# A DLRM tower on one core: the order of turns and lookups, who rounds the table halves, and how ids are compared

## The reference, cut to what matters

```python
e = jnp.stack([tbl_0[ids[:, 0]], ..., tbl_25[ids[:, 25]]], axis=1)
T = jnp.concatenate([r_dense[:, None, :], e], axis=1)          # 2048 x 27 x 128
Z = jnp.einsum('bnd,bmd->bnm', T, T)
z = Z[:, iu0, iu1]                                             # 351 pairs above the diagonal
h = jnp.concatenate([z, r_dense], axis=1)
h = jnp.maximum(h @ W_top1 + b_top1, 0.0)                      # 512
h = jnp.maximum(h @ W_top2 + b_top2, 0.0)                      # 256
y = h @ W_top3
```

## Time and profile before

| | us |
|---|---|
| median of 3 runs | 503.87 |
| lowest, highest | 503.16, 509.52 |
| the profiled execution's own time | 503.01 |
| its span, first to last instruction | 501.2 |
| PE busy (matmul) | 394.7 (79%) |
| POOL busy | 251.3 (50%) |
| DVE busy | 221.8 (44%) |
| ACT busy | 175.2 (35%) |
| mean granted TensorE clock | 0.884 of 2.4 GHz |

### The profile page before, as it was taken

The page is one execution under the profiler, slowest core; times in us unless marked ns, Lnnn a source line. Parts: engine busy times, 40 slices in busy tenths (PEclk is TensorE's granted clock), DMA queues, the critical chain, the costliest instruction groups (busy, mean ns, idle before and its releaser), DMA issues.

```text
span 501.2 us, 9930 instructions
## 1 busy us (share of the span) xinstructions
PE 394.7 (79%) x4044; PEld 348.3 (69%) x4044; DVE 221.8 (44%) x815; ACT 175.2 (35%) x220; POOL 251.3 (50%) x263
## 2 busy tenths in 40 slices
PE   5848357696498968987689868989679866999998
PEld 3727356595397837976489746978479754988987
DVE  5616642586263404823365404734247223744321
ACT  4121550354135312363215512354214522344231
POOL 6747573637545554447635563546653475360000
PEclk9958596888599969999699976999599996999999
DMA  8926130115501422115311332114321251013221
GB/s 216 245 60 192 48 105 24 52 48 128 171 25 47 97 71 90 38 33 140 102 27 38 81 100 85 33 43 105 99 60 28 50 130 47 24 47 67 49 51 22
DMA packets 45878, 39.07 MB, mean 78 GB/s; under 512 B 32930, under 2 KB 39113, under 8 KB 45834
## 3 DMA queue, kind: packets, MB, share of 16 engines
q1 hardware_dynamic: 36014, 21.40, 16.4%
q0 software_dynamic: 8192, 16.79, 13.0%
q10 hardware_dynamic: 1628, 0.25, 0.3%
HBM read 32.40 MB, written 6.02 MB: 77 GB/s over the span
## 4 chain that ended last, share of the span: by engine, by line
PE 52%; another core or an unknown queue 27%; DVE 11%; ACT 4%; issue 4%; DMA 1%; DVEq 0%; SPq 0%; ACTq 0%
PE look_ps L763 24%; PE gram_ps L790 9%; PE mlp_ps L810 7%; DVE hot L474 7%; PE look_ps L773 5%; ACT T L625 3%; PE mlp_ps L820 3%; PE look_ps L754 1%; DVE gram L497 1%; DVE tab_lo L456 1%; PE look_ps L831 1%; PE look_ps L853 1%; DMA ids_all<-in_ids_dram 1%; DVE gram L445 0%
## 5 line engine op out<-in xcount | busy, mean ns | idle before, releaser
L425 POOL DMA_INDIRECT rows<-in_tbl_dram,ids_all x240 | 233.9, 975 | 193.3 <-PE look_ps L773 104.5
L474 DVE TENSOR_SCALAR hot<-ids_near 125x256 fp32r<-125x256 f16 x640 | 146.0, 300 | 142.8 <-remote 98.7
L763 PE MATMUL look_ps<-hot,tab_hi 125*128 125x256 f32 x616 | 160.6, 298 | 29.1 <-DVE hot L474 11.1
L763 PE MATMUL look_ps<-hot,tab_lo 125*128 125x256 f32 x616 | 156.4, 291 | 6.8 <-issue 6.0
L763 PEld LDWEIGHTS look_ps<-hot,tab_hi 125*128 125x128 f32 x616 | 122.1, 198 | 33.0 <-issue 26.6
L763 PEld LDWEIGHTS look_ps<-hot,tab_lo 125*128 125x128 f32 x616 | 122.5, 199 | 8.5 <-issue 8.5
L625 ACT COPY T<-look_ps 128x384 f32<-128x384 f32 (+1 forms) x80 | 83.4, 1076 | 113.0 <-PE look_ps L773 96.8
L790 PE MATMUL gram_ps<-T 128*54 128x54 f32 x2048 | 72.7, 224 | 39.3 <-issue 30.1
L790 PEld LDWEIGHTS gram_ps<-T 128*54 128x54 f32 x2048 | 64.3, 138 | 51.3 <-issue 39.6
L617 ACT COPY T<-look_ps 128x512 f32<-128x512 f32 x32 | 38.5, 1204 | 100.9 <-PE look_ps L763 53.5
L497 DVE COPY gram<-gram_ps 128x486 f32<-128x486 f32 (+1 forms) x64 | 37.9, 607 | 77.3 <-remote 52.7
(11 more groups left out here) (74 smaller groups left out, 151.4 us busy)
## 6 DMA issues: line engine op xcount, KB each, us to landing
dots<-gram SPq DMA_DIRECT2D x28, 182.2 KB
ids_near<-ids_rows SPq DMA_DIRECT2D x7, 640.0 KB
rows<-in_tbl_dram,ids_all POOLq DMA_INDIRECT x240
T<-in_tbl_dram SPq DMA_DIRECT2D x5, 448.0 KB
pairs<-dots SPq DMA_DIRECT2D x14, 117.0 KB
rows<-in_r_dense_dram SPq DMA_DIRECT2D x16, 64.0 KB
gram<-in_tbl_dram SPq DMA_DIRECT2D x2, 448.0 KB
pairs<-dots SPq DMA_DIRECT2D x7, 104.0 KB
```

What stands on the lines that cost most here:

```text
L425: pool.indirect_dma_start(rows[:, t % 2, place[n], :], None, tables[n - 1], bass.IndirectOffsetOnAxis(ap=index[:, n - 1:n].bitcast(U32), a ...
L474: eq = nc.vector.tensor_scalar(hot[:VP, at % 2, c], ids_near[:VP, u % 2, k], float(c), None, ALU.is_equal)
L763: mm = pe.matmul(dst, w[:VP, k, c], hot[:VP, slot, c], start=(c == 0 and half == 0), stop=(c == CH - 1 and half == 1))
```

## The change

Three edits.

1. In `first_half`, ACT's loop and PE's loop, for u > 0: turn(u,1,2) now comes between look(u+1,0) and look(u+1,1), turn(u,1,3) between look(u+1,1) and look(u+1,2), and turn(u,1,4) after layer1 steps 0 to 8. Unit 0's order is unchanged, but for the casts.
2. `lead`, `top` and its semaphore are gone. ACT casts raw to `tab_hi` itself (its write rounds), in the order LEADING and sooner; DVE subtracts `tab_hi` from raw. There are five raw slots in place of three, so eight tables load at once, and the small weights load later.
3. For units 2 and up, places 0, 6, 7, 8 and 9 are compared by one TENSOR_TENSOR of 8x256 elements against eight chunk numbers kept in PSUM (columns 500 to 507 of `gram_ps`'s second bank, memset once). So that PE doesn't write that bank meanwhile, piece 1 of products(u, l) waits for the compares before it.

```diff
+    LEADING = (0, 1, 2, 3, 4, 6, 5, 7, 8, 9)
-        raw_slots = [table_at(spare, 0), table_at(spare, CH * D), table_at(gram_flat, 2 * CH * D)]
+        raw_slots = [table_at(spare, i * CH * D) for i in range(2)] + [table_at(gram_flat, i * CH * D) for i in range(3)]
+        steps = gram_ps[:, 1, 500:500 + CH]
+        def by_steps(u, at):
+            return u >= 2 and at in (0, 6, 7, 8, 9)
         def first_half(u):
             if u > 0:
-                return [("turn", u, 1, 0), ("turn", u, 1, 1), ("look", u + 1, 0), ("look", u + 1, 1),
-                        ("turn", u, 1, 2), ("look", u + 1, 2), ("turn", u, 1, 3), ("turn", u, 1, 4)]
+                return [("turn", u, 1, 0), ("turn", u, 1, 1), ("look", u + 1, 0), ("turn", u, 1, 2),
+                        ("look", u + 1, 1), ("turn", u, 1, 3), ("look", u + 1, 2), ("turn", u, 1, 4)]
...
-            for k in range(6):
+            for k in range(8):
                 load_raw(k)
             load_dense(0, 0)
-            load_raw(6)
-            load_small_weights()
-            load_raw(7)
+            load_raw(8)
...
+            def split(k):
+                dve.wait_ge(hi_ready, hi_count(k))
                 for c in range(0, CH, 2):
                     minus = nc.vector.tensor_tensor(tab_lo[:VP, k, c:c + 2], raw[k][:VP, c:c + 2],
-                                                    top[2 if k in WHOLE else i % 2][:VP, c:c + 2], ALU.subtract)
+                                                    tab_hi[:VP, k, c:c + 2].bitcast(F32), ALU.subtract)
...
+                if by_steps(u, at):
+                    if u == 2 and at == 0:
+                        dve.wait_ge(steps_ready, CH)
+                    near = ids_near[:VP, u % 2, k:k + 1].to_broadcast([VP, CH, Q])
+                    eq = nc.vector.tensor_tensor(hot[:VP, at % 2], near, steps[:VP].rearrange(
+                        "p (c q) -> p c q", q=1).to_broadcast([VP, CH, Q]), ALU.is_equal)
...
             def hi_out(k):
-                i = split_count(k) - 1
-                act.wait_ge(top_ready, i + 1)
-                nc.scalar.copy(tab_hi[:VP, k], top[2 if k in WHOLE else i % 2][:VP]).then_inc(hi_ready, 1)
+                act.wait_ge(raw_landed[k], 32)
+                nc.scalar.copy(tab_hi[:VP, k], raw[k][:VP]).then_inc(hi_ready, 1)
...
+                if t == 0 and b == 0:
+                    pe.wait_ge(steps_ready, CH)
+                if b == 1 and 0 < u < END:
+                    pe.wait_ge(hot_ready, K * (u + 1) + (1 if l == 0 else 8))
...
                 turn(u, 1, 1)
                 look(u + 1, 0)
+                turn(u, 1, 2)
+                look(u + 1, 1)
+                turn(u, 1, 3)
                 if u > 0:
-                    look(u + 1, 1)
-                    turn(u, 1, 2)
                     look(u + 1, 2)
                     layer1(u - 1, 0, 8)
-                    turn(u, 1, 3)
-                    layer1(u - 1, 8, 12)
                     turn(u, 1, 4)
-                    layer1(u - 1, 12, 16)
+                    layer1(u - 1, 8, 16)
```

More of the change, by code:

```diff
@@ L95, in dlrm_tower @@
     assert VP * CH == V and VP <= P and V <= 2048 and D == P and F1C == 4 and F2C == 2 and K % 2 == 0
-    assert NV % 2 == 1 and MC * PC == NV and KP <= P and 18 * NV <= 512 and dense_round == NR - 1
+    assert NV % 2 == 1 and MC * PC == NV and KP <= P and 18 * NV <= 500 and dense_round == NR - 1
     w1_pieces = pair_weight_pieces(NV, HALF, MC)
@@ L150, in dlrm_tower @@
         in_turn = [k for k in range(K) if k not in WHOLE]
-        raw = [whole_raw[WHOLE.index(k)] if k in WHOLE else raw_slots[in_turn.index(k) % 3] for k in range(K)]
-        top = [table_at(gram_flat, 0), table_at(gram_flat, CH * D)]
+        raw = [whole_raw[WHOLE.index(k)] if k in WHOLE else raw_slots[in_turn.index(k) % len(raw_slots)] for k in range(K)]
         look_ps = psum("look_ps", [P, RING, 512], F32)
@@ L187, in dlrm_tower @@
         dense_ready = sem("dense_ready")
+        steps_ready = sem("steps_ready")
         gram_done = sem("gram_done")
@@ L307, in load_raw @@
             def load_raw(k):
-                if k not in WHOLE and in_turn.index(k) >= 3:
-                    sp.wait_ge(lo_ready, in_turn.index(k) - 2)
+                if k not in WHOLE and in_turn.index(k) >= len(raw_slots):
+                    sp.wait_ge(lo_ready, in_turn.index(k) - len(raw_slots) + 1)
                 src = tables[onehot[k]].rearrange("(p c) d -> p c d", c=CH)
@@ L472, in compare @@
                     dve.wait_ge(hot_looked, K * u + at - 1)
-                for c in range(CH):
-                    eq = nc.vector.tensor_scalar(hot[:VP, at % 2, c], ids_near[:VP, u % 2, k], float(c), None,
-                                                 ALU.is_equal)
+                if by_steps(u, at):
[4 more added lines that the diff above has]
+                        "p (c q) -> p c q", q=1).to_broadcast([VP, CH, Q]), ALU.is_equal)
+                else:
+                    for c in range(CH):
+                        eq = nc.vector.tensor_scalar(hot[:VP, at % 2, c], ids_near[:VP, u % 2, k], float(c), None,
+                                                     ALU.is_equal)
                 eq.then_inc(hot_ready, 1)
@@ L545, in _ @@
                 compare(0, at)
+            dve.wait_ge(ids_t_ready, UNITS)
+            for c in range(CH):
+                nc.vector.memset(steps[:, c:c + 1], float(c)).then_inc(steps_ready, 1)
             compare(1, 0)
@@ L555, in _ @@
                 if u == 0:
+                    split(WHOLE[0])
                     dense_out(u, 1)
[L557 to L562, removed]
+                compare(u + 1, 6)
+                compare(u + 1, 7)
+                if u > 0:
                     dense_out(u, 1)
@@ L565, in _ @@
                 if u == 0:
-                    lead(WHOLE[1])
-                    compare(u + 1, 7)
-                    rest(WHOLE[1])
+                    split(WHOLE[1])
                 compare(u + 1, 8)
                 if u == 0:
-                    lead(WHOLE[2])
+                    split(WHOLE[2])
                 compare(u + 1, 9)
-                if u == 0:
-                    rest(WHOLE[2])
                 if u + 2 < UNITS:
@@ L667, in _ @@
                 spread_out(j)
-            hi_out(0)
+            for k in LEADING[:5]:
+                hi_out(k)
             look_out(0, 0)
-            hi_out(2)
             for g in range(4):
```

62 lines of the change are left out of this document (18 added, 44 removed).

## The result

The changed kernel takes 532.44 us (median of 4 runs, 530.51 to 536.64); the kernel before, beside it, 506.69 (503.16 to 511.29). The ratio is 1.051, with a 95% interval of 1.043 to 1.059: slower, as forecast, and 5.4 us above the 527 us of the prediction. Ratios here leave out executions that took over 1.5% more than the fastest of their kernel; medians keep them. The profiled execution took 530.51 us, with a span of 528.7 us and a mean granted clock of 0.848, where it was 0.884.

What follows compares the result with a forecast made beforehand. Prediction: no engine is full; PE's signals come late while POOL gathers without a pause. Profiled 503.0 + 26 (turns) - 1.4 (compares) - 1 (split) = 526.6, forecast 527 us; own range 515 to 535, 8 in 10 488 to 537.

Steps and rivals of the forecast that it cites:

- Edit 1: First half of units 1 to 6: sooner turns join POOL's rounds 1 and 2; +4.3 us a unit, +26 us, bounds -18 and +38.
- X: Start of POOL's round 1 in a unit's first half, 255.44 us in the forecast's trace; later times count from it.
- the products' 3.0 us: Lateness of the signal for the products' first copy, first half; forecast to go, already inside the +4.3 us a unit.
- unit 0's unknown wait: Unit 0, before the fifth compare: 5.96 us idle behind eight gathers; the forecast took unit 0's times as price.
- Edit 3: Five TENSOR_TENSOR compares: +0.4 to 0.5 us each, hidden; gathers beside compares get faster, 0.24 us a run, -1.4 us in all.
- The covers: Compares of places 6 and 7 hide behind layer1, 8 and 9 under the 14-gather run; without cover, 2 us a unit.
- Edit 2: Start of the kernel: `lead` leaves DVE, which waits for late signals anyway; -1 us, bounds -4 and +2.
- The sum: Whole kernel: 503.0 + 26 - 1.4 - 1 = 526.6 us, forecast as 527 us, 4.6% slower.
- A: Third lookup's signal, first half: not late in the new order, only the products' 3.0 us go; 484 us, chance 0.17.
- B: First half: signal late, but the clock holds and POOL pauses sooner; 508 to 512 us, no tellable change, chance 0.20.
- C: Second half: 2-port compares cause the late signals, so removing them gains 10 us or more a unit; 445 us, chance 0.05.
- D: Place 4's late compare delays y and layer1; slow clock covers layer1 and part of the products; 540 us, chance 0.08.

Runs made afterwards that it cites:

- split and compares: Changed kernel without the sooner turns (ACT rounds leading parts, five compares by TENSOR_TENSOR), against the kernel before, chip 9: 513.85 us, ratio 1.0147.
- the split alone: Kernel before with only ACT rounding the leading parts and five raw slots: 515.80 us, ratio 1.0167 on chip 9; 357.25 us, 0.9841 on chip 4.

## Why the prediction was right, and where it was not

**The verdict, the sign and the cause held.** The forecast was 527 us with slower as the likeliest, from one mechanism: eight gathers in a row in the first half, and the third table's signal late because of them. The run without gathers takes away all late signals behind the start, and the hold on POOL, with the turns left in their new places, takes away two thirds of their loss and puts the third table's signal back in its old place. Both bear out the mechanism on chips like that of the forecast's trace.

**Edit 1** was priced at +4.3 us a unit, X to the products' first copy going from 23.3 to 27.6 us. In unit 3 it went to 295.18 - 268.84 = 26.3 us, +3.0; the mean of units 1 to 6 is 25.9, +2.6. By its own steps in unit 3: the fifth compare was due at X + 11.5 and came at X + 10.0; the couple was to take 6.55 us and took 6.41; the products' 3.0 us were to go and went. The 1.5 us too many came from taking unit 0's unknown wait as it stood. This wait came in two sizes: some 4.5 us in five of the six units and 5.9 in one, but 5.7 to 5.9 in four of the six in the turns alone. The unit as a whole lost 3.8 us, so about 1 of it lies outside that stretch. Six units at 3.8 are 23 us for the 26 of the forecast. The turns alone, on chip 9, cost 19.4 us by the medians (529.22 - 509.85), 3.2 a unit.

**Edit 3** was priced at -1.4 us. The instruction takes 2.29 us for the 2.2 forecast. The 14-gather run, from its first start to its last, went from 16.49 us (282.09 to 298.58) to 16.26 (298.50 to 314.76), about the 0.24 forecast. The covers held as well. Places 8 and 9 are compared under the run, from 300.69 us. The late compare, at 316.52 us, is that of place 0 of the next unit; it takes 0.58 us more (2.29 - 1.71), but DVE then still waits 0.80 us for ACT's dense vector, as it waited 0.67 before, so this is on no path either. Whether the 1.4 us came can't be told: with split and compares against the split alone the ratios are 1.0147 and 1.0167. No run has the compares alone on such a chip; on chip 4 they lose 0.3%.

**Edit 2** is the step that failed: "I take -1 us; bounds -4 and +2". On the forecast's own two traces it is +5.7 us at tile 4, and alone on chip 9 it costs 1.67%, some 8 us. The text had a right ground for no gain, that DVE waits there for late signals anyway. But the term was written down as one of work, with bounds from work, and the start was never walked through as the loop was: neither where POOL pauses there nor when the stored ids release it. Both moved; which of them made the loss is open.

**The sum**, 23 + 6 from 503.0 us, is 532; the profiled execution took 530.5. A term too large by 3 and one too small by 7 left 4 us against the 526.6 of the text. On chip 9 it is the same by medians: +19.4 for the turns and +8.2 for the split. So that the number came within 5.4 us is in part luck, two errors that pull against each other.

**The rivals.** A (484 us, the lateness is unit 0's own) falls: the fifth compare is late in all of units 1 to 6, by a wait of 4.5 us or more. B (508 to 512, POOL pauses sooner and the clock holds) falls by the clock of 0.59 and by the missing pause; only with POOL held by hand did the kernel come to 511.65. C (445 us, the 2-port compares are the cause) falls: five of ten compares left that form, and the long wait is 11.35 us for 12.61, and 0.72 of this difference is that the two compares in front of it take 4.49 us for 3.77; and where all ten compares keep it but 240 gathers are gone, no signal is late behind the start. The Trainium skill (SBUF — State Buffer, "Who interferes with whom") says that such a compare and a GpSimd instruction lock each other out, whichever comes second, and that PE never waits. The traces agree in direction: most gathers beside the old compares take about 1.02 us for 0.95, in five units of the changed kernel one takes 2.4, and the 34 beside the new compares all take 0.95. But these are delays of POOL's, and it is PE's signals that are late, with or without the old compares. D (540 us, the slow clock covers layer1) falls in unit 3, where layer1 takes 3.46 us for 16 matmuls, at the fast clock.

## What to carry to other kernels

Before a step is moved sooner, ask what it releases: here a turn that was done sooner let another engine's gathers close up into one run, and that cost 4%, where the turn's new place gives 0.4% on a chip without late signals. A pattern read from one chip's trace can be right there and absent on another; when a quarter of the chain is "unknown", measure on more than one chip before tuning to it. And a term that is priced by the work it removes must still be asked whether it moves a pause.

## What the runs showed of the hardware

The same program takes 362.4 us on chip 4 and 508 to 516 on the others, some 29% less, with the same work: PE 4044 matmuls, POOL 256 gathers. Edits 1 and 2 change sign between them (0.9955 and 0.9841 against 1.0396 and 1.0167). The changed kernel itself was not run on chip 4.

On the other chips it is not only signals that come late: PE's own instructions drip, too. Under the run of 14 gathers of the kernel before, PE's lookups run at full pace until 291 us; from 292 us single matmuls follow each other with idle time between them that no wait explains, until 300.6 us, a microsecond after the run:

```profile
293.50 0.38 PE L773 MATMUL look_ps<-ident,rows 128*128 128x128 f32 x2 [1.02 <-issue]
```

Two timelines of PE beside POOL's first run of gathers, the changed kernel and then the split alone on chip 4, the same 16 matmuls of one look:

```profile
22.63 0.38 PE L740 MATMUL look_ps<-hot,pairs 125*128 125x256 f32 x1 [1.62 <-issue]
24.73 0.59 PE L740 MATMUL look_ps<-hot,pairs 125*128 125x256 f32 x1 [1.72 <-issue]
26.13 0.58 PE L740 MATMUL look_ps<-hot,pairs 125*128 125x256 f32 x1 [0.82 <-issue]
```

```profile
18.32 3.62 PE L740 MATMUL look_ps<-hot,pairs 125*128 125x256 f32 x16
```

In the changed kernel a matmul starts every 1.4 to 2.1 us; PE is back at its pace at 35 us, some 3.5 us after POOL's last gather of that run has ended (31.70). On chip 4 all 16 take 3.62 us beside the same gathers. The idle time is put down to "issue", so PE waits for nothing that the profile shows. Why the gathers do this to PE, and what differs between the chips, stays open: no run here tells it.
